# Step sizes of the next group on GpSimd, inverse norms on ScalarE, all matrices on VectorE

## The reference, cut to what matters

```python
dt = jnp.clip(jax.nn.softplus(dt_raw + dt_bias), DT_MIN, DT_MAX)      # 1e-4 .. 0.1
Bm = _l2norm(bc[..., 0, :])      # t / sqrt(sum(t * t) + 1e-8), the same for Cm
def step(carry, inp):
    denom = 1.0 + dt_t[:, :, None] * kdamp + dt_t[:, :, None] ** 2 * A
    v = (v - dt4 * A[None, :, None, :] * y + dt4 * u_t[..., None] * Bv_t[:, :, None, :]) / denom[:, :, None, :]
    y = y + dt4 * v + dt4 * u_t[..., None] * By_t[:, :, None, :]
    o = jnp.einsum('bhpn,bhn->bhp', y, Cy_t) + jnp.einsum('bhpn,bhn->bhp', v, Cv_t)
```

## Time and profile before

| engine | busy us | share of the span | instructions |
|---|---|---|---|
| TensorE (matmuls) | 444.1 | 81% | 3238 |
| TensorE (weight loads) | 358.6 | 66% | 3238 |
| VectorE | 469.8 | 86% | 1275 |
| ScalarE | 252.1 | 46% | 489 |
| GpSimd | 306.3 | 56% | 373 |

### The profile page before, as it was taken

The page is one execution under the profiler, slowest core; times in us unless marked ns, Lnnn a source line. Parts: engine busy times, 40 slices in busy tenths (PEclk is TensorE's granted clock), DMA queues, the critical chain, the costliest instruction groups (busy, mean ns, idle before and its releaser), DMA issues. The chain is left out here.

```text
span 545.8 us, 9581 instructions
## 1 busy us (share of the span) xinstructions
PE 444.1 (81%) x3238; PEld 358.6 (66%) x3238; DVE 469.8 (86%) x1275; ACT 252.1 (46%) x489; POOL 306.3 (56%) x373
## 2 busy tenths in 40 slices
PE   5850159996979988896889968898789987998997
PEld 4740147885747667784657757687565766786886
DVE  5699989989999998989989998989989997789542
ACT  1551126563375525453546524454537542444363
POOL 2027867768508757668526657676553676778100
PEclk9995559998999969999979988998988997999999
DMA  7500000000000010000000000000000000000000
GB/s 224 153 0 0 1 1 2 1 2 1 0 1 1 1 40 1 1 1 2 1 0 2 0 21 1 1 2 2 0 1 0 2 0 21 2 1 1 2 11 10
DMA packets 8434, 7.06 MB, mean 13 GB/s; under 512 B 1593, under 2 KB 7618, under 8 KB 8258
## 3 DMA queue, kind: packets, MB, share of 16 engines
q1 hardware_dynamic: 8386, 6.46, 3.9%
HBM read 5.41 MB, written 1.05 MB: 12 GB/s over the span
## 5 line engine op out<-in xcount | busy, mean ns | idle before, releaser
L590 PE MATMUL BC<-xnT,winT 128*128 128x128 f32 x512 | 79.8, 306 | 50.8 <-ACT pr L893 29.7
L590 PEld LDWEIGHTS BC<-xnT,winT 128*128 128x128 f32 x512 | 70.4, 214 | 58.2 <-issue 31.0
L1616 POOL TENSOR_TENSOR big<-mm 128x256 f32<-128x256 f32 x64 | 50.3, 786 | 71.4 <-DVE mm L1345 71.4
L1648 POOL TENSOR_SCALAR uT<-uT,skipT 128x512 f32<-128x512 f32 x8 | 17.0, 2138 | 73.9 <-DVE w L1430 42.1
L1619 POOL TENSOR_TENSOR vt<-mm 128x256 f32<-128x256 f32 x64 | 58.1, 907 | 0.0
L542 PE MATMUL HB<-xnT,w 128*128 128x512 f32 x108 | 55.7, 645 | 1.9 <-ACT gtm L978 0.9
L1637 POOL TENSOR_TENSOR mm<-ab,pr 128x256 f32<-128x256 f32 x48 | 41.3, 881 | 20.4 <-ACT pr L893 20.2
L915 ACT ACTIVATE big<-GV 128x256 f32<-128x256 f32 x60 | 23.1, 385 | 62.3 <-PE GV L615 60.9
L612 PE MATMUL GV<-big,vt 128*128 128x128 f32 x256 | 44.0, 297 | 8.3 <-POOL vt L1619 8.3
L1343 DVE TENSOR_TENSOR mm<-BC,pr 128x512 f32<-128x512 f32 x64 | 44.2, 691 | 5.7
L612 PEld LDWEIGHTS GV<-big,vt 128*128 128x128 f32 x256 | 35.8, 202 | 14.1 <-POOL vt L1619 11.6
(11 more groups left out here) (225 smaller groups left out, 1179.1 us busy)
## 6 DMA issues: line engine op xcount, KB each, us to landing
xr<-in_x SPq DMA_DIRECT2D x4, 256.0 KB, 4.5
winT<-in_w_inT SPq DMA_DIRECT2D x1, 1024.0 KB, 5.6
w<-in_rw SPq DMA_DIRECT2D x1, 1024.0 KB
out<-xr SPq DMA_DIRECT2D x3, 256.0 KB, 2.6
taps<-in_dw_wT SPq DMA_DIRECT2D x1, 512.0 KB, 3.6
w<-in_sw SPq DMA_DIRECT2D x2, 128.0 KB
out<-xr SPq DMA_DIRECT2D x2, 128.0 KB, 1.8
winT<-in_w_inT SPq DMA_DIRECT2D x1, 130.0 KB, 2.7
```

The source lines that it names most:

```text
L590: last = pe.matmul(b[:, j * TS:(j + 1) * TS], winT[:, col:col + NS], xt, start=True, stop=True)
L1616: pool.tensor_tensor(wt[q % 8][:], m[:, 0], m[:, 3], ALU.add)
```

## The change

It has three parts.

1. Step sizes of the next group. For groups 1 to 3 VectorE's instructions at `F_EXP` and `F_LOG1P` go to GpSimd, in a new `front_early` there, called behind `ubar` and `gates` and ahead of `wv` of the same step. The polynomial's fused instruction becomes two (an addition and a product), so there are 2 + 19 dependent instructions in place of 2 + 11. The logits, the exponential and the logarithm move one step earlier (k = 4, 5, 6 for 5, 6, 7); the rows stay at k = 8. Group 0's step sizes stay on VectorE.
2. Inverse norms. `norms_copy` on ScalarE becomes the logarithm of the sum plus epsilon and an exponential with a scale of -0.5. The power on GpSimd goes. ScalarE waits for `ub_done` of the tile before. The load of the table with exponential and logarithm moves from `F_EXP` to k = 0 of the middle phase, in all four groups; the load at the end of group 3's pairs goes.
3. Matrices. GpSimd's four instructions a group go; VectorE makes all 20 for every group with one function.

```diff
-MAT_OPS = 14
+MAT_OPS = 20
...
-    0, 2, 3, 5, 6, 7, 8, 9, 13, 15, 17)
+    0, 2, 3, 4, 5, 6, 8, 9, 13, 15, 17)
...
                 if k == F_EXP:
-                    if g:
-                        act.preload_act_table_set("natural_log_exp_and_others")
                     act.wait_ge(dt_e, g + 1)
                     act.activation(le, lx, ACT.Exp).then_inc(dt_exp, 1)
...
             def norms_copy(tile):
                 hb = h_read("norms", tile)
+                act.activation(nsq[:], view(hb, 0, (TS, 2), (32, NH)), ACT.Ln, bias=eps_l2[:]).then_inc(h_free, 1)
                 if tile:
-
-                    act.wait_ge(inv_done, tile)
-                act.activation(nsq[:], view(hb, 0, (TS, 2), (32, NH)), ACT.Identity, bias=eps_l2[:]).then_inc(h_free, 1)
+                    act.wait_ge(ub_done, tile)
+                act.wait_ge(h_free, h_read_of("norms", tile))
+                act.activation(rinv[:], nsq[:], ACT.Exp, scale=-0.5).then_inc(inv_done, 1)
...
                     if k < KP:
                         pair(KP * g + k)
-                        if KP * g + k == NT * NH - 1:
+                        if k == 0:
                             act.preload_act_table_set("natural_log_exp_and_others")
...
-                if k == F_EXP:
+                if g == 0 and k == F_EXP:
...
-                if k == F_LOG1P:
+                if g == 0 and k == F_LOG1P:
...
-                    if g >= 2:
-                        dve.wait_ge(ub_done, GT * (g - 1))
                     dve.tensor_scalar(dtts[g % 2][:], lp[0], DT_MIN, DT_MAX, ALU.max, ALU.min).then_inc(dt_done, 1)
...
+                    dve.wait_ge(mat_d, MAT_OPS * g + n)
...
                 if part == 0:
                     dve.wait_ge(ab_done, g + 1)
-
-                    dve.wait_ge(wv_done, KP * g)
-                    dve.wait_ge(h_ready, h_read_of("sums", GT * g - 1))
+                    if g:
+
+                        dve.wait_ge(wv_done, KP * g)
+                        dve.wait_ge(h_ready, h_read_of("sums", GT * g - 1))
                     for f in range(2):
                         dve.tensor_tensor(scr(f, 0), c1(f, 0), c2(f, 0), ALU.mult).then_inc(mat_d, 1)
-                    dve.tensor_tensor(scr_x(1), c1(1, 1), c2(1, 0), ALU.mult).then_inc(mat_d, 1)
+                    for f in range(2):
+                        dve.tensor_tensor(scr_x(f), c1(f, 1), c2(f, 0), ALU.mult).then_inc(mat_d, 1)
                 if part == 1:
                     for f in range(2):
                         after(1 + f)
                         dve.tensor_scalar(scr(f, 1), scr(f, 0), -1.0, 1.0, ALU.mult, ALU.add).then_inc(mat_d, 1)
-                    after(3)
-                    dve.tensor_scalar(entry(1, "x", "x"), scr_x(1), -1.0, 1.0, ALU.mult, ALU.add).then_inc(mat_d, 1)
                     for f in range(2):
-                        after(4 + f)
+                        after(3 + f)
+                        dve.tensor_scalar(entry(f, "x", "x"), scr_x(f), -1.0, 1.0, ALU.mult, ALU.add)\
+                            .then_inc(mat_d, 1)
+                    for f in range(2):
+                        after(5 + f)
                         dve.tensor_tensor(scr(f, 0), c1(f, 1), scr(f, 1), ALU.mult).then_inc(mat_d, 1)
-                    after(6)
-                    dve.tensor_tensor(scr_x(1), c2(1, 1), entry(1, "x", "x"), ALU.mult).then_inc(mat_d, 1)
+                    for f in range(2):
+                        after(7 + f)
+                        dve.tensor_tensor(scr_x(f), c2(f, 1), entry(f, "x", "x"), ALU.mult).then_inc(mat_d, 1)
...
-                    dve.wait_ge(mat_e, 2 * g)
-
-                    dve.wait_ge(mat_p, g)
...
-            first_matrices()
+            for part in range(3):
+                matrices(0, part)
...
-            def matrices(g):
-
-                pool.wait_ge(ab_done, g + 1)
-                pool.wait_ge(h_ready, h_read_of("sums", GT * g - 1))
-                link(pool.tensor_tensor(scr_x(0), c1(0, 1), c2(0, 0), ALU.mult))
-                link(pool.tensor_scalar(entry(0, "x", "x"), scr_x(0), -1.0, 1.0, ALU.mult, ALU.add))
-                link(pool.tensor_tensor(scr_x(0), c2(0, 1), entry(0, "x", "x"), ALU.mult))
-                pool.tensor_tensor(entry(0, "v", "x"), c2(0, 0), scr_x(0), ALU.add).then_inc(mat_p, 1)
-
...
+            def front_early(g, k):
+                if k == F_EXP:
+
+                    pool.wait_ge(h_free, h_read_of("logits", g))
+                    link(pool.tensor_tensor(lx.rearrange("p (c h) -> p c h", c=GT),
+                                            lraw.rearrange("p (c h) -> p c h", c=GT),
+                                            view(dtbb, 0, (0, GT), (1, NH)), ALU.add))
+                    pool.tensor_scalar(lx, lx, 0.0, None, ALU.min).then_inc(dt_e, 1)
+                if k == F_LOG1P:
+
+                    pool.wait_ge(dt_exp, g + 1)
+                    link(pool.tensor_scalar(le, le, E_MAX, None, ALU.min))
+                    link(pool.tensor_scalar(lp[0], le, 1.0 / 9, None, ALU.mult))
+                    for i, m in enumerate(range(8, 0, -1)):
+                        c = (1.0 if m % 2 else -1.0) / m
+                        link(pool.tensor_scalar(lp[1], lp[0], c, None, ALU.add))
+                        link(pool.tensor_tensor(lp[0], lp[1], le, ALU.mult))
+                    pool.tensor_scalar(dtts[g % 2][:], lp[0], DT_MIN, DT_MAX, ALU.max, ALU.min).then_inc(dt_done, 1)
+
...
-                pool.wait_ge(h_free, h_read_of("norms", tile))
-                pool.tensor_tensor(rinv[:].rearrange("p i h -> p (i h)"), nsq[:].rearrange("p i h -> p (i h)"),
-                                   mhalf[:], ALU.pow).then_inc(inv_done, 1)
                 pool.wait_ge(inv_done, tile + 1)
...
+                    if g + 1 < NG:
+                        front_early(g + 1, k)
...
-                    matrices(g + 1)
```

## The result

The changed kernel takes 560.29 us, the median of six executions (558.86 to 561.95), the kernel before beside it 549.72 (549.52 to 549.85): ratio 1.0185, 95% interval 1.0155 to 1.0216. It is slower, by 10.6 us; 7.6 were forecast. The profiled execution took 558.86 us with a span of 557.1, 11.3 more than before.

The account below looks back on a forecast made before the run. TensorE's queue was taken to bound k = 7 to about 11, VectorE the rest until the matrices. Stall 8.4 + clock 4.9 - norms 3.1 - matrices 2.6 = 7.6 us more, on the median 557.3 us; range 548.5 to 562.0 (8 in 10).

Parts of the forecast that it names:

- The bound and the place: Middle phase: TensorE's queue sets the pace from k = 7 to about 11, then VectorE; lateness at k = 7 paid in full.
- The block: GpSimd at k = 6, ahead of wv(6): 19 small instructions at 0.30 us, 5.6 us a group, bounds 4.7 and 6.5.
- The collision with the state update: Groups 1 and 2, k = 6: VectorE's state update holds up GpSimd's small instructions by 0.7 us, between nothing and 1.9.
- TensorE's pause and its clock: Ahead of gv(6): TensorE idle 3.5 to 4.3 us a group, then a lower clock costing 1.6 each, 4.9 us in all.
- Rival (a): At gv(6): the stall is as said but the granted clock stays up; 552.4 us, chance 0.27.
- The relief of VectorE at k = 7: Step sizes off VectorE spare TensorE's waits: 1.77 us each in groups 1 and 2, only 0.16 in group 0.
- The inverse norms: GpSimd loses 16 powers; TensorE's group 3 waits of 2.0 and 1.1 us go, 3.1 us gained, bounds 1.5 and 6.6.
- The matrices: Passages between groups: VectorE's wait for GpSimd goes; 1.1 us gained in group 0, 0.75 in 1 and 2: 2.6, bounds 0 and 4.
- The sum: Whole kernel: stall 8.4 plus clock 4.9, less norms 3.1 and matrices 2.6, makes 7.6 us more: 557.3 us.
- (b): At gv(6): the 19 instructions fit into power and slack, 2.65 us, and relief wins; 540.5 us, chance 0.12 with milder forms.
- (c): At k = 6: all three state instructions lost, 1.2 us more in two groups, and 0.35 us an instruction; 562.4 us, chance 0.10.
- (d): On ScalarE: logarithm and exponential load tables in turn, 1.28 us each time; 578 us if half is covered, chance 0.03.

Follow-up runs that it names:

- the pause filled: Full change plus 34 (group 0) and 40 (groups 1 and 2) unused TensorE transposes ahead of gv(6); 554.01 us, ratio 1.0074.
- the short portions: Full change with degree-5 polynomial, 11 GpSimd instructions split 4, 4, 3 over k = 6 to 8, and GpSimd waiting for the state update; 536.47 us, ratio 0.9776.
- Part 2 alone: Kernel before with ScalarE's logarithm and exponential in place of GpSimd's power, the rest unchanged; 550.76 us, ratio 1.0017.
- The wait that keeps the two apart: GpSimd waits for VectorE's state update before wv: without the step-size move 543.36 us, 0.988; in the full change (not at k = 6, groups 0 to 2) 551.89, 1.0065.
- parts 2 and 3: Full change with the step sizes of all groups left on VectorE as before; 546.33 us, ratio 0.9961.
- the short polynomial: Full change with a polynomial of degree 5 instead of 9, 11 GpSimd instructions at k = 6 instead of 19; 544.76 us, ratio 0.9918.

## Why the prediction was right, and where it was not

**The bound and the place: right.** Lateness of TensorE at k = 7 was to be paid in full and kept until after k = 16. The shift of q = 9, 5.5 us, is still 4.9 at q = 15 and 9.2 at q = 31.

**The block: right in kind, 0.6 us short a group.** 19 instructions were told with 0.30 us each and 5.6 us in all; they take 0.325 and 6.2. For the larger tile I had counted 0.01 us in all; the difference is 0.025 an instruction. My bounds of 4.7 and 6.5 hold it. The two-input one took 0.22 us busy, 0.31 from start to start. By the ratio of 1.96 in the Trainium skill's GPSIMD Engine Reference, section "Performance versus the Vector engine", it would have been 0.51, an estimate; at this size, 16 elements, the trace decides against that ratio.

**The collision with the state update: right in kind.** 0.7 us were taken of a span of 0 to 1.9; it was 1.0 (7.2 against 6.2). Three small instructions took 0.57, 0.53 and 0.65 us instead of 0.25: short ones get in between long ones, each held up a little. The Trainium skill, SBUF — State Buffer, section "Who interferes with whom", has the second comer blocked for the whole of the other's instruction; the trace agrees as far as it goes: the first small one started at 221.91, 0.2 us behind VectorE's of 0.68 us, and ended at 222.48, 0.1 behind its end. But in the 2.0 us of VectorE's three instructions three of the block's got done, so that the full 1.9 us did not come.

**TensorE's pause and its clock: right, the pause longer than told.** Pauses of 3.96, 5.00 and 5.22 us (3.5 to 4.3 told), and behind each some 4 us at 0.51 to 0.57. The price of 1.6 us a group, taken from one stretch of before, was 1.6, 1.8 and 1.6 with the pause filled. Rival (a), the clock stays up, fell with this; it would have given 552.4 us.

**The relief of VectorE at k = 7: counted about right.** Block, collision and clock less the relief were 5.0 us in group 0 and 4.1 in groups 1 and 2, and the middle phases lost 4.9, 5.2 and 5.2: 15.3 instead of 13.3, a difference that the longer block (1.8) and the collision (0.6) cover. The relief itself is seen where the block is small: q = 23 to 25 takes 7.6 us before and 5.9 with the short portions, 1.8 less for the 1.77 told. The agreement by phases is rougher than it looks: at the stall itself 5.5, 4.9 and 4.7 us are lost, behind it part 2 gives back 0.6 each (q = 9 to 15 and so on), and at the start of the phases of groups 1 and 2 (q = 16 to 23, 32 to 39) 1.0 and 1.2 us are lost, where more half clock lies than before (6.8 us of it instead of 3.4 and 5.5). For this the prediction had no term, and whether the change puts it there is not shown.

**The inverse norms: wrong.** The step that failed is "these 3.1 us go", with its bounds of 1.5 and 6.6. The waits for the power and the scaled input did go, but I asked only who waits for GpSimd, not what GpSimd would now run beside. In group 3 the power was also what kept wv away from the state update, and 3.2 us of waits for the state came in the place of the 3.1. Part 2 alone measured 0 (0.9988 to 1.0047), and in the full change group 3 lost 1.3 us instead of gaining 3.1. The wait that keeps the two apart gives 3.0 us on parts 2 and 3, 6.6 in the full change, and turns group 3's loss of 1.3 us into a gain of 1.6. Half of the 3.1 was thus there to be had; the rest stays open. The text's own rows held the hint: the collision was priced at k = 6 and for no other tile.

**The matrices: right in kind, half the gain.** 2.6 us told, 0.9952 measured, 2.6; but that the two are the same is in part luck. Where the gain was told, in the passages, it was 4.7 us alone (0.7, 1.8 and 2.2; 1.5 were lost elsewhere, at q = 35) and 5.3 in the full change, against 1.1, 0.75 and 0.75 told. The chain there (between groups 2 and 3 of the changed kernel):

```profile
412.49 1.11 DVE L1101 TENSOR_SCALAR xn<-xr,mv,rstd 128x128 f32<-128x128 f32 x4
...
416.87 1.06 PE L526 MATMUL HB<-rw,xnT 128*128 128x8 f32 x8 [0.69 <-ACT xnT L950]
...
418.19 0.19 DVE L1352 TENSOR_TENSOR lg<-lg,rb 128x32 f32<-128x32 f32 x1 [0.85 <-ACT lg L955]
```

The router's matmuls of the kernel before, to be read against the row of 416.87:

```profile
405.98 1.88 PE L527 MATMUL HB<-rw,xnT 128*128 128x8 f32 x8 [0.69 <-ACT xnT L952]
```

The normalisation starts 9.0 us after its start before (403.47), while q = 47 was 12.3 late: 3.3 gained, where 2.7 were told. The logits then come 10.1 after 408.13: 1.0 us of it is lost again to the router's logits, as told, but 2.3 stay instead of 0.75. My cap of 1.35 us, TensorE's idle time ahead of its transpose, held for that idle time: the transpose starts 1.4 us earlier against q = 47. What it left out is the clock. Before, the idle time was followed by 0.50 from 405.9 to 412.8 us, and the router's matmuls took 1.88 us; in the changed kernel the clock stays at 1.00 and they take 1.06. 1.4 and 0.8 are the 2.3. In group 1 they took 1.59 before, in group 0 1.06, which orders the gains of 2.0 and 0.9 in the same way; in every profiled kernel with part 3 they take 1.06 in all three.

**The sum.** Told 8.4 + 4.9 - 3.1 - 2.6 = 7.6. In the profile: middle phases +15.3, passages -5.3, group 3 and the end +1.3, together +11.3; the median rose by 10.6. The forecast of 557.3 is 3.0 us low, within its range of 548.5 to 562.0. Against the terms, the profile has 2.0 more in the middle phases, 2.7 more gained in the passages and 4.4 worse in group 3. The first two cancel in part (the longer block and collision against the passages), and the forecast comes this close with a wrong term for the norms partly by luck. Of the rivals, (b) was refused by the first pause, but its condition was tested: when block and clock together shrink, in the short polynomial, the kernel is faster than before (0.9918). (c) got a quarter of its dearer collision and half of its dearer instruction. Of (d) nothing shows: part 2 alone costs no time.

## What to carry to other kernels

A chain of small instructions is cheap by its sum and dear by its place: 19 in a row ahead of what TensorE needs next cost 12 us against leaving them on VectorE (1.0185 against 0.9961), the same 19 in three portions 3, and 11 in three portions nothing that could be measured. When work is taken off an engine, look at what that engine will then run beside: a slow instruction that reads little can keep two large ones apart, and two that meet can be worth a wait even where the change did not bring them together. And a pause of the matrix engine is to be costed twice, as its length and as what the clock may take behind it; a pause that goes can give that back.

## What the runs showed of the hardware

The clock is not a matter of the pause's length alone. In these traces pauses of 1.36 and 1.40 us were followed by a granted clock of 1.00, one of 2.41 by 0.58, but one of 2.62 in the same kernel by 1.00; and the pauses of 3.96, 5.00 and 5.22 us by 0.56, 0.51 and 0.57. In the kernel before TensorE waits 1.77, 1.78 and 1.77 us for the state at 126.09, 251.63 and 378.29, and the 4 us from there have 0.57, 1.00 and 0.57. What else decides, these runs don't show. Work that nobody reads kept the clock up: 34 transposes in 3.93 us.

GpSimd's power of 8 elements a partition takes 1.67 us and does not stretch a two-input instruction of VectorE beside it. Group 3 of the kernel before, the power and the middle one of VectorE's three:

```profile
467.02 1.67 POOL L1663 TENSOR_TENSOR rinv<-nsq,mhalf 128x8 f32<-128x8 f32 x1
...
468.21 0.69 DVE L1364 TENSOR_TENSOR x<-tr,zz 128x512 f32<-128x512 f32 x1
```

A sum of GpSimd over 256 elements, on the other hand, stretches VectorE's of 512 from 0.68 to 1.21 us and is itself stretched from 0.73 to 1.17. Side by side the state update (2.08 us alone, the three means with the wait) and wv (1.46 alone) last 3.1 us, from 477.58 to 480.70: being at it at once saves 0.4 us of 3.5.
